# One cast of the lanes for two chunks, in the sum by source of a four-layer graph network

## The reference

```python
def _L0_gnn_ref(x, edge_row, edge_col, edge_val, weight, gamma, beta):
    ...
    support = x @ hamilton
    msg = edge_val[:, None] * support[edge_col]
    out = jax.ops.segment_sum(msg, edge_row, num_segments=x.shape[0])
    mean = jnp.mean(out, axis=0)
    ...
    return jnp.tanh(y)

h = jnp.maximum(_layernorm(x, axis=-1), 0.0)
x = x + _L0_gnn_ref(h, src, dst, edge_weight, L0_gnn_weight, L0_gnn_gamma, L0_gnn_beta)
```

## Time and profile before

| | us |
|---|---|
| median of 3 runs | 9899.29 (9899.1 to 9899.61) |
| the profiled execution, its own time | 9879.09 |
| its span, first to last instruction | 9877.3 |
| the sum by source, first cast to last matmul | 2442.0 to 2887.7 |

### The profile page before, as it was taken

One profiled execution on the slowest core, in us unless ns is written; L12 is line 12 of the kernel. 1 busy time (PEld: TensorE's weight loads), 2 busy tenths in 40 slices (PEclk: granted clock), 3 DMA queues, 4 the chain that ended last, 5 costly groups with the idle time before them and its releaser, 6 DMA issues. The chain is left out here.

```text
span 9877.3 us, 180292 instructions
## 1 busy us (share of the span) xinstructions
PE 6940.7 (70%) x25668; PEld 5290.0 (54%) x25669; DVE 5689.7 (58%) x22975; ACT 2075.3 (21%) x8101; POOL 6853.4 (69%) x7052
## 2 busy tenths in 40 slices
PE   2676766665757888888835555555567888888885
PEld 2555555554545666666633333333345666666664
DVE  8777777776984444444455555555554444444443
ACT  4344444442110000000002222222221222222222
POOL 0677777776756777777747777777735777777772
PEclk8555555555555555555555555555565555555556
DMA  6333333333852222222212222222202333333333
GB/s 110 93 109 104 104 104 104 106 103 110 267 178 59 55 55 55 57 55 55 56 37 53 53 55 53 53 53 55 53 20 74 82 79 81 81 82 79 81 81 24
DMA packets 441030, 782.96 MB, mean 79 GB/s; under 512 B 192009, under 2 KB 220329, under 8 KB 439854
## 3 DMA queue, kind: packets, MB, share of 16 engines
q1 hardware_dynamic: 209502, 487.65, 17.3%
q0 software_dynamic: 216064, 278.76, 12.8%
q10 hardware_dynamic: 14544, 8.74, 0.5%
HBM read 634.79 MB, written 139.85 MB: 78 GB/s over the span
## 5 line engine op out<-in xcount | busy, mean ns | idle before, releaser
L1213 POOL DMA_INDIRECT arena<-node_table,idx x3328 | 3153.7, 948 | 1127.5 <-issue 819.1
L1151 PE MATMUL banks<-arena,onehot 128*128 x7040 | 2482.5, 470 | 1273.1 <-DVE onehot L1099 613.8
L1151 PEld LDWEIGHTS banks<-arena,onehot 128*128 128x128 f32 x7040 | 1756.0, 311 | 1895.5 <-issue 1687.3
L913 POOL DMA_INDIRECT sorted_edges<-arena,idx x1664 | 1625.9, 977 | 616.4 <-issue 576.5
L1334 POOL DMA_INDIRECT arena<-node_table,arena x1760 | 1660.6, 944 | 565.6 <-issue 370.9
L1099 DVE TENSOR_SCALAR onehot<-iota_row,block_base,edge_tables 128x128 f32<-128x128 f32 x3520 | 1251.6, 358 | 635.8 <-ACTq L1197 502.2
L858 PE MATMUL banks<-arena,onehot 128*128 x3520 | 1117.7, 428 | 569.7 <-DVE onehot L807 557.2
L858 PEld LDWEIGHTS banks<-arena,onehot 128*128 128x128 f32 x3520 | 882.5, 313 | 795.9 <-issue 792.0
L1107 DVE TENSOR_TENSOR arena<-arena,banks 128x65 f32 (+1 forms) x3520 | 893.7, 254 | 605.5 <-PE banks L1151 562.6
L1310 PE MATMUL banks<-arena 128*128 128x64 f32 x3520 | 1215.3, 449 | 0.0
L1305 PE MATMUL banks<-arena 128*64 128x65 f32 x3520 | 844.3, 343 | 390.1 <-ACT arena L1321 378.3
(11 more groups left out here) (288 smaller groups left out, 6194.7 us busy)
## 6 DMA issues: line engine op xcount, KB each, us to landing
arena<-sorted_edges SPq DMA_DIRECT2D x440, 524.0 KB, 4.5
arena<-in_attr_t SPq DMA_DIRECT2D x208, 512.0 KB, 3.6
arena<-row_keys SPq DMA_DIRECT2D x110, 512.0 KB, 4.9
arena<-in_attr_pairs SPq DMA_DIRECT2D x104, 512.0 KB
arena<-node_table,idx POOLq DMA_INDIRECT x3328, 2.4
arena<-node_table,arena POOLq DMA_INDIRECT x1760, 2.4
sorted_edges<-arena,idx POOLq DMA_INDIRECT x1664, 2.4
node_table<-arena SPq DMA_DIRECT2D x3, 3136.0 KB, 12.6
```

The source lines that it names most:

```text
L913: nc.gpsimd.indirect_dma_start(m.sorted, bass.IndirectOffsetOnAxis(ap=m.idx[:, j % (4 * CH):j % (4 * CH) + 1], axis=0), m.out_ring[:, slot ...
L1151: nc.tensor.matmul(to, m.onehot[:, j % 4, :], rows, start=True, stop=True).then_inc(s["summed"], 1)
L1213: nc.gpsimd.indirect_dma_start(slot(j), None, m.table, bass.IndirectOffsetOnAxis(ap=m.idx[:, j:j + 1], axis=0)).then_inc(gathered[j % 32], 16)
```

## The change

VectorE no longer casts the lanes chunk by chunk. At each even chunk it waits for its own load and for the next chunk's load, and casts the lanes of both in one operation of 16 elements per partition. Where the pair lies in slots 4 and 0 of the ring (c = 4 and c = 14), it does two casts of 8 elements, one directly after the other. At odd chunks it neither waits for a load nor casts. Nothing else differs; the other engines have the same instructions.

```diff
+            def keep_lanes(c, count):
+                first = c % DEEP
+                to = m.lanes16[:, first:first + count, :].rearrange("p c s -> p (c s)").unsqueeze(2)
+                return v.tensor_copy(to, rings[:, 0, first * CB:(first + count) * CB, REC_LANE:REC_LANE + 1])
+
             with dve.Fori(0, BODIES) as i:
                 for c in range(chunks):
                     n = i * chunks + c
-                    dve.wait_ge(rec_in[c % DEEP], arrived(i, c))
+                    lanes = m.lanes16[:, c % DEEP, :]
 
                     dve.wait_ge(s["summed"], n * CB + CB)
-                    lanes = m.lanes16[:, c % DEEP, :]
-                    v.tensor_copy(lanes.unsqueeze(2), rings[:, 0, tiles(c), REC_LANE:REC_LANE + 1]).then_inc(s["lanes"], 1)
+                    if c % 2 == 0:
+                        dve.wait_ge(rec_in[c % DEEP], arrived(i, c))
+                        dve.wait_ge(rec_in[(c + 1) % DEEP], arrived(i, c + 1))
+                        if c % DEEP == DEEP - 1:
+                            keep_lanes(c, 1).then_inc(s["lanes"], 1)
+                            keep_lanes(c + 1, 1).then_inc(s["lanes"], 1)
+                        else:
+                            keep_lanes(c, 2).then_inc(s["lanes"], 2)
                     v.tensor_tensor(value(c, 1), value(c, 0), part(c, 0), ALU.subtract).then_inc(s["rest"], 1)
-                    dve.wait_ge(s["lanes"], n + 1)
+                    dve.wait_ge(s["lanes"], i * chunks + c // 2 * 2 + 2)
```

## The result

The changed kernel takes 9931.04 us (median of 7 runs, 9927.21 to 9933.28), the one before 9898.57 (7 runs, 9895.99 to 9899.61). The ratio is 1.0033, with a 95% interval of 1.0021 to 1.0045: slower, by 32.5 us. The profiled execution took 9930.71 us.

A forecast was written before the change was run, and what follows sets the result against it. VectorE was taken to bound the stage, TensorE close behind. The new load loop, 3.63 + 0.22 + 4.5 + 0.2 = 8.55 us per four chunks, adds 26 us, GpSimd 2: 9899.3 + 28 = 9927 us, range 9892 to 9955.

The forecast's parts named there:

- The loop through the load: Even cast waits for a load released by TensorE's earlier matmuls: 8.55 us per four chunks, stage 26 us longer; chance 0.58.
- The waits before casts: VectorE idle before even chunks' casts, released by the DMA: about 110 times, 0.4 to 0.6 us, some 50 us.
- The saving of 17.6 us: VectorE: 88 fewer casts at 0.20 us each, the upper bound of the gain.
- GpSimd's windows: GpSimd's additions need 196 windows beside VectorE's casts and get 110, each 0.43 us wider; 2 us taken as cost.
- the cast is its only window: GpSimd gets its operands only beside VectorE's casts, not during subtractions and comparisons; VectorE loses about 0.12 us per window.
- the second rival: GpSimd starves: 86 of 196 additions left without a window, +50 us and up to 12 more; chance 0.14.
- additions would end in pairs within the gaps: Sign of the loop: GpSimd's additions end in pairs in the idle gaps before even casts, some at 299 ns.
- TensorE's floor: TensorE's matmul groups go no faster than about 1.98 us per chunk: 440 us for the stage, some 5 us gainable.
- The third rival: Loads land sooner, so VectorE or TensorE is again the bound: 0 to 5 us shorter, about 9896 us; chance 0.22.
- point of decision: Issue to landing of a load: at or below 4.03 us the loop is no longer than four chunks before.
- the forecast of +28 us: Whole kernel: 26 us from the load loop plus 2 us from late GpSimd additions, nothing else moving; 9927 us.

The follow-up runs named there:

- e1: Kernel before with its 220 casts, but at even chunks VectorE also waits for the next chunk's load: stage 477.6 us (445.7 before), whole ratio 1.0033.
- e4: Changed kernel with only half of each chunk's records loaded: stage 444.0 us, whole ratio to before 1.0011.
- e11: Kernel before with bank numbers of two chunks in one load and GpSimd's additions replaced by fills that read nothing: stage 424.4 us.
- e12: Kernel before with GpSimd's additions replaced by fills, TensorE's loads of bank numbers unchanged: stage 446.3 us.
- e5: Kernel before, unchanged, run again on another chip: stage 445.8 us.
- e6: Kernel before, but TensorE's queue loads 16 bank numbers at even chunks, not 8 at each: stage 445.9 us, whole ratio 0.9999.
- e2: Kernel before without the casts at odd chunks, each chunk waiting for its own load alone: stage 446.1 us, whole ratio 1.0006.
- e9: Changed kernel with the wait for the next load and the pair's cast between the two subtractions: stage 454.7 us, whole ratio to before 1.0021.
- e3: Changed kernel with the wait for the next load and the pair's cast behind the even chunk's first subtraction: stage 459.9 us, ratio to before 1.0020.

## Why the prediction was right, step by step

**The loop through the load.** Right, in kind and, for the stage, in size. Four chunks were to take 8.55 us and take 473.1 / 55 = 8.60. By terms, in the piece of timeline shown: subtraction to end of the matmuls 3.75 (3.63 was taken), issue 0.22 (0.22), issue to the next subtraction 4.71 (4.5 + 0.2). e1 shows that the wait alone is enough, e4 that with a short landing the loss is gone. Three terms were off and nearly cancel: additions that pass within the loop cost 0.08 us of it on the mean (3.71 and not 3.63), 4 us in all and not the 2 that were taken; what is left of a loop besides the three terms is 0.25 us and not 0.2, 3 us in all; and the loads landed 0.1 us sooner, 6 us in all, for which nothing was taken. The waits before casts were to come about 110 times with 0.4 to 0.6 us, some 50 us; they come some 80 times and are 38 us. The large operations became 23 + 29 + 17 = 69 ns longer, 15 us over 220 chunks, and take a part of what was to be waiting.

**The saving of 17.6 us** was mis-sized. 0.20 us per cast is what a cast and the addition that passes beside it cost together; the cast itself is 0.08 (e11, e12), so 7 us for 88 casts, and e1 against the changed kernel gives 4.5. The 0.12 us per addition did not go away with the casts: they are the 15 us by which the large operations grew. This error was without effect, since the loop set the pace.

**GpSimd's windows.** The step "the cast is its only window" failed. It holds for the kernel before, on two chips (in e5 195 of 196 additions end beside a cast), but with a wait added or moved or a cast gone most additions pass between two large operations and end about 0.24 us after the start of the second, which is lengthened by about 0.1 us (2473.59 in the timeline above, 0.82 and not 0.68 us). So the second rival, that GpSimd starves, did not come true: the additions became shorter in every kernel that changed VectorE's waits or casts, and stayed as they were in e5 and e6, which change neither. The sign that additions would end in pairs within the gaps was not borne out either: most do not end in a gap. What decides who gets in stays open.

**TensorE's floor.** I had 440 us and so 5 us of room. I had also put the 0.45 us ahead of a group down mostly to "issue", while the earlier trace rows give 124.5 of the 186.3 us to VectorE; e12, where VectorE has time to spare, keeps the same gap, so as a floor it was right. e2, e4 and e12 end at 446.1, 444.0 and 446.3: the room was 0 to 2 us. Its groups start 1.98 us apart at the median, as I had taken, but 2.00 on the mean: it meets more delays than the one at the end of a body. Which, no run shows.

**The third rival,** the loads landing sooner, was wrong about the loads: they are 0.1 us quicker on the median with more room between them, 4.4 us, not 4.0. Its point of decision was not tested closely: the loss is there at 4.4 us and gone at 2.7 (e4), on either side of 4.03. The formula that the prediction took from the Trainium skill (DMA: Bandwidth & Descriptors, Anatomy of one DMA) is given there for one transfer on GpSimd's path, and these loads go through SyncE's queue, one every 2 us. By it half a load would take 2.6 us, an estimate, near e4's 2.7, but a whole one 3.2 where 4.4 to 4.5 were measured.

**The rest of the time.** 32.5 - 27.4 = 5 us are outside the stage, within the interval, and the forecast of +28 us had nothing for them. That the whole came so near is therefore in part luck. But in the experiments the whole differs from before by 8 to 28 us more than the stage does wherever VectorE's instructions of this stage are other ones (in e9, 35.8 us for the whole and 9.0 for the stage), and by nothing in e6, where they are the same. The intervals are 13 to 18 us to either side, yet the sign is the same in all eight, so a part of it may be real. Where it lies stays open: outside the stage, the profiled executions of e5 (the kernel before) and of e6 already differ by 23 us.

## What to carry to other kernels

Before two steps of a ring are merged, go round the ring: what the instruction now waits for is itself released by this engine's work a few steps back, so a wait that looks like half a microsecond of lateness closes a loop, and the loop's length sets the pace from then on. Compare the length of that loop (work, issue, landing, wake-up) with the engine's own work for as many steps; here a loop of 8.55 us against a former pace of 8.08, 0.47 us in four chunks, was enough to foretell 26 us. And such a wait is cheap or dear by where it stands: 0.61 us later in the chunk it cost 13 us less in the stage (e3), and a part of what was left came from the order of the operations. And what an instruction seems to cost in an engine that is always busy may be another engine's passage beside it: it comes back elsewhere when the instruction goes.

## What I had not expected of the hardware

- In the kernel before, in e5 and in e6, all but 3 of GpSimd's 588 additions end beside a cast, and line 1020's take 1.9 us on the mean; in all other kernels with additions the means by line are 0.53 to 0.98 us and most pass between two large operations of VectorE, though they start, as before, in the middle of one. The Trainium skill (SBUF — State Buffer, Who interferes with whom) says that the two share a pair of ports as an exclusive lock, and of VectorE's two-port modes that whoever issues first gets the pair for the whole instruction and the other blocks. The trace agrees that one blocks (1.95 us for an addition that takes 0.30 at its shortest), but no run here shows why in the kernel before mostly two large VectorE operations start ahead of a waiting addition before it gets in, and in the others mostly one operation starts during a whole addition.
- A VectorE operation that waits by a semaphore for the one directly before it, and reads what that one wrote, starts 0.12 us later than otherwise (0.73 and not 0.61, 0.20 and not 0.08), even where the first has only 8 or 16 elements. No run separates the wait from the reading.
- With all loads halved, a load lands after 2.7 us and not 4.4. The DMA engines' busy share fell with it from 0.81 to 0.49, so whether a single half load among whole ones would gain the 1.7 us is not shown.
